# A three-layer kernel on eight cores: another beginning, and six other places at which work is issued

## The reference, cut to what matters

```python
x = L0_attn_hidden_states                     # (4, 4096, 2048) float32
x = x + 0.5 * ffn(layernorm(x))
x = x + attn(layernorm(x))
x = x + 0.5 * ffn(layernorm(x))               # the same weights again

def ffn(x):                                   # D = 2048, K = 8, R = 64
    h = relu(x @ W1 + b1)
    alpha = softmax(h @ W2 + b2)              # 8 weights for each token
    vx = einsum('krd,bsd->bskr', V, x)
    uvx = einsum('kdr,bskr->bskd', U, vx)
    return einsum('bsk,bskd->bsd', alpha, uvx)

def attn(x):                                  # 16 heads of 128
    q, k, v = heads(x @ Wq), heads(x @ Wk), heads(x @ Wv)
    scores = q @ k.T * 128 ** -0.5 + mask     # 0 where |block i - block j| <= 2, blocks of 64; else -1e30
    return merge(softmax(scores) @ v) @ Wo
```

## Time and profile before

| | |
|---|---|
| three runs | 1987.72, 1796.43 and 1979.18 us, median 1979.18 |
| the profiled execution, its own time | 1798.14 us |
| its span (core 0, the slowest) | 1796.6 us |
| spans of the eight cores | 1774.4 to 1796.6 us |
| busy, share of the span | PE 96%, PEld 64%, DVE 44%, ACT 23%, POOL 12% |
| stages on core 0 | first: to 438 us; attention: to 1225; output: to 1449; last: to 1797 |

### The profile page before, as it was taken

One profiled execution on the slowest core, in us unless ns is written; L12 is line 12 of the kernel. 1 busy time (PEld: TensorE's weight loads), 2 busy tenths in 40 slices (PEclk: granted clock), 3 DMA queues, 4 the chain that ended last, 5 costly groups with the idle time before them and its releaser, 6 DMA issues.

```text
span 1796.6 us, 34598 instructions; the slowest of 8 cores (1774.4 to 1796.6 us)
## 1 busy us (share of the span) xinstructions
PE 1726.2 (96%) x12544; PEld 1140.8 (64%) x12544; DVE 786.1 (44%) x1631; ACT 404.8 (23%) x998; POOL 222.4 (12%) x373
## 2 busy tenths in 40 slices
PE   3999899899799999999999999999999999999998
PEld 3876655455577777777777777775444455575555
DVE  5036475344455454545454555545213333153421
ACT  2311311111133333333333333332000011111111
POOL 2001121121111111111111111121000110011000
PEclk9999899999899999999999999999999999999999
DMA  9947877989957574757565556678681553264321
GB/s 210 180 91 229 209 251 176 201 156 182 106 83 103 74 107 76 105 80 94 83 93 94 81 84 81 117 175 254 213 315 49 144 161 127 57 182 129 104 78 55
DMA packets 288583, 242.07 MB, mean 135 GB/s; under 512 B 219808, under 2 KB 260768, under 8 KB 277536
## 3 DMA queue, kind: packets, MB, share of 16 engines
q1 hardware_dynamic: 238096, 121.27, 31.2%
q0 software_dynamic: 44848, 100.19, 29.0%
q10 hardware_dynamic: 5472, 18.40, 3.2%
HBM read 164.74 MB, written 77.07 MB: 135 GB/s over the span
## 4 chain that ended last, share of the span: by engine, by line
PE 85%; DMA 6%; DVE 4%; SPq 2%; issue 1%; ACT 1%; POOL 0%; DVEq 0%; ACTq 0%; POOLq 0%
PE R L745 25%; PE R L390 16%; PE R L735 13%; PE R L1027 12%; PE R L472 4%; PE pX L390 4%; PE R L443 4%; PE R L892 2%; DMA xnTa<-xna 2%; DVE lnb L310 2%; SPq L102 2%; DMA Xa<-x 2%; DMA W1a<-w 2%; PE pX L472 1%; PE pX L852 1%; PE pS L852 1%
## 5 line engine op out<-in xcount | busy, mean ns | idle before, releaser
L735 PE MATMUL R<-wvS,xn2T 128*128 128x256 bf16 x2176 | 253.4, 274 | 6.2 <-ACT Kb L752 6.2
L745 PE MATMUL R<-xn2T,wkS 128*128 128x384 bf16 (+1 forms) x1536 | 251.5, 317 | 0.0
L745 PE MATMUL R<-xn2T,wqS 128*128 128x384 bf16 (+1 forms) x1536 | 239.1, 309 | 0.0
L735 PEld LDWEIGHTS R<-wvS,xn2T 128*128 128x128 bf16 x2176 | 213.2, 98 | 37.5 <-issue 6.5
L390 PE MATMUL R<-xnTa,W1a 128*128 128x256 bf16 (+2 forms) x1632 | 209.1, 288 | 28.5 <-DMA xnTa<-xna 12.6
L1027 PE MATMUL R<-Wo,Ob 128*128 128x512 bf16 x1024 | 222.2, 379 | 0.0
L745 PEld LDWEIGHTS R<-xn2T,wkS 128*128 128x128 bf16 x1536 | 150.1, 98 | 82.1 <-issue 0.6
L745 PEld LDWEIGHTS R<-xn2T,wqS 128*128 128x128 bf16 x1536 | 150.4, 98 | 74.5 <-issue 1.2
L390 PEld LDWEIGHTS R<-xnTa,W1a 128*128 128x128 bf16 x1632 | 142.6, 101 | 77.3 <-issue 34.3
L390 PE MATMUL R<-xnTc,W1c 128*128 128x384 bf16 (+1 forms) x1232 | 185.3, 308 | 0.0
L1027 PEld LDWEIGHTS R<-Wo,Ob 128*128 128x128 bf16 x1024 | 100.1, 98 | 119.6
(11 more groups left out here) (94 smaller groups left out, 1664.1 us busy)
## 6 DMA issues: line engine op xcount, KB each, us to landing
y<-Xc SPq DMA_DIRECT2D x16, 1024.0 KB, 3.9
x1d<-Xa SPq DMA_DIRECT2D x14, 1024.0 KB, 4.3
Xa<-x POOLq DMA_DIRECT2D x10, 1024.0 KB, 10.6
Xc<-x1d POOLq DMA_DIRECT2D x9, 1024.0 KB, 14.9
W1a<-w POOLq DMA_DIRECT2D x16, 512.0 KB, 44.2
w1b<-W1a ACTq DMA_DIRECT2D x16, 512.0 KB, 9.4
wkS<-wk POOLq DMA_DIRECT2D x64, 128.0 KB, 3.6
wqS<-wq POOLq DMA_DIRECT2D x64, 128.0 KB, 4.0
```

Of the source, the lines that this page charges most:

```text
L735: tok = p.mm(lambda e, c=c, o=o: e.matmul(bank[:, 0:256], xn2T[:, o:o + 128], wvS[s][:, c * 256:(c + 1) * 256], start=(c == 0), stop=(c == ...
L745: tok = p.mm(lambda e, c=c: e.matmul(bank[:, 0:w], wS[:, c * 256 + k * 128: c * 256 + (k + 1) * 128], view(xn2T, a * D + c * 128, (D, n), ...
```

## The change

- The beginning. Tile 0 is requested in two halves, and SP requests only tiles 0 and 1. POOL waits for the first half, then requests W1 part 0, W2, tile 2, W1 part 1, tile 3, W1 part 2, tile 4 and the other W1 parts. Tile 0's statistics wait for each half by itself, and its apply and its transpose go by halves (`apply_halves`). All five tiles are normalized first in DVE's list. The pieces of block 0 are written out: each tile is turned in PE's list where it comes, with pieces of one tile for the W1 parts that are there, and pieces of two and three. From e = 5 on the block has two sub-blocks, of three and of two tiles.
- An Exp of one column on ACT is issued at the very beginning.
- Block 1. Tile 0 is normalized a second time during block 0's U matmuls, on ACT (`ln2_act`), and x 7 is requested then. Tile 7 is turned by DMA, not by PE, after item 6 rather than 13. The hooks of block 1 have a new order; tile 10 is normalized on ACT after item 27 and turned after item 29, not during the V matmuls. Four `copy_w1` are issued here.
- Blocks 2 and 3: eight `copy_w1` in block 2 as before, four in block 3, after items 0, 2, 4 and 6, in place of eight.
- The start of attention: one memset of part of `Pn[0]`, ahead of the second normalization of tiles 14 and 15, in place of three whole ones behind it; tile 16's second normalization and transpose one group later, and tile 14's and 15's transposes without it between.
- Loads during attention: in pair 0 the next pair's slab parts come in groups 2 to 5, six in each, rather than in groups 1 to 5; no `cast_wo` in pair 0, six in each of pairs 1 to 6 (before five in each of 0 to 6).
- The last stage's groups 1 and 2 change places.

```diff
-BLOCKS = [[(0, 1), (1, 2), (3, 2)], [(5, 2), (7, 1)], [(8, 3)], [(11, 3)], [(14, 3)]]
+BLOCKS = [[(0, 3), (3, 2)], [(5, 2), (7, 1)], [(8, 3)], [(11, 3)], [(14, 3)]]
...
+    p.op("scalar", lambda e: e.activation(warm[:, :], mhalf[:, :], AF.Exp), cst["mhalf"])
...
-                    st[:, j * 6:j * 6 + 6], x[:, j * 512:(j + 1) * 512]), token, *free)
+                    st[:, j * 6:j * 6 + 6], x[:, j * 512:(j + 1) * 512]),
+                    token[j // 2] if isinstance(token, list) else token, *free)
...
+        def apply_halves(self, x, st_tok):
+            st, stok = st_tok
+            b, free = self.xn.take()
+            toks = [p.op("vector", lambda e, o=o: e.tensor_scalar(
+                b[:, o:o + 1024], x[:, o:o + 1024], st[:, 24:25], st[:, 26:27],
+                ALU.subtract, ALU.mult), stok, *free) for o in (0, 1024)]
+            ln_sets.give(st, toks[1])
+            return b, toks
...
-                    8, [tok])
+                    8, [tok[half] if isinstance(tok, list) else tok])
...
-    for t in range(5):
-        load_x(t, "sync")
+    x0_tok = [p.dma("sync", S(f"dxa{h}_x0"), xa(0)[:, h * 1024:(h + 1) * 1024],
+                    rows(dx, 0)[:, h * 1024:(h + 1) * 1024]) for h in range(2)]
+    load_x(1, "sync")
     W1atok = []
+    p.wait("gpsimd", x0_tok[0])
     for e in range(16):
         W1atok.append(p.dma("gpsimd", S(f"w1a{e}"), W1a[e][:, :], rows(dw1, e)))
         if e == 0:
             cst["w2p"] = p.dma("gpsimd", S("c_w2p"), W2b[:, :], dw2[:, :])
+        if e < 3:
+            load_x(e + 2, "gpsimd")
...
-        if t < 5 or t == 7:
+        if t < 5:
             xnT_tok[t] = norm.turn(*norm_b[t], xnTa, place[t], free)
...
+    def ln2_act(t, new):
+        st = norm.shift(*norm.stats(xa(t), x_add[t], minus=True))
+        ln2_b[t] = b, tok = norm.apply_act(xa(t), st)
+        x_free[t % 7] = (tok, x1_tok[t])
+        load_x(new, "gpsimd")
...
-    for t in range(3):
+    st0 = norm.stats(xa(0), x0_tok)
+    norm_b[0] = norm.apply_halves(xa(0), st0)
+    for t in range(1, 5):
         ln1(t)
         flush_ln()
-    ln1_turn(0)
-    ln1(3)
-    flush_ln()
-    items = [(0, 0), (0, 1), (0, 2)]
-    items += [(1, e) for e in range(3)] + [(s, e) for e in (3, 4) for s in (0, 1)]
-    items += [(2, e) for e in range(5)]
-    items += [(s, e) for e in range(5, 16) for s in range(3)]
-    hooks = at_hooks([(1, call(ln1_turn, 1)), (1, call(ln1, 4)), (1, flush_ln), (2, call(ln1_turn, 2)),
-                      (7, call(ln1_turn, 3)), (9, call(ln1_turn, 4)),
-                      (36, call(ln1, 5)), (39, call(ln1, 6)), (41, flush_ln)])
-    run_items(0, items, hooks)
-    vu_a(0, at_hooks([(("v", 1), call(ln1_turn, 5)), (("v", 2), call(ln1_turn, 6))]))
+    items = [(0,), (0, 1, 0), (1,), (1, 1, 0), (0, 2, 1), (2,), (2, 1, 0), (2, 1, 1), (0, 3, 2),
+             (3,), (0, 3, 3), (3, 1, 0), (3, 1, 1), (3, 1, 2), (4,), (0, 3, 4),
+             (4, 1, 0), (4, 1, 1), (4, 1, 2), (3, 2, 3), (3, 2, 4)]
+    items += [(t, n, e) for e in range(5, 16) for t, n in ((0, 3), (3, 2))]
+    late = {len(items) - 8: call(ln1, 5), len(items) - 4: call(ln1, 6), len(items) - 2: flush_ln}
+    for i, item in enumerate(items):
+        if len(item) == 1:
+            ln1_turn(item[0])
+        else:
+            t, n, e = item
+            first.w1(0, t, n, place[t], e, [xnT_tok[q] for q in range(t, t + n)])
+        if i in late:
+            late[i]()
+    vu_a(0, at_hooks([(("v", 1), call(ln1_turn, 5)), (("v", 2), call(ln1_turn, 6)),
+                      (("u", 0), lambda: ln2_act(0, 7))]))
...
-    for t in range(3):
-        ln2_load(t, 7 + t)
-    flush_ln()
+    ln1_half(7)
+    ln2_load(1, 8)
+    ln2_load(2, 9)
...
-        (4, call(ln2_store, 0)), (7, call(ln2_store, 1)), (9, call(ln2_store, 2)),
-        (9, call(ln1_half, 7)), (10, call(ln2_load, 3, 10)), (10, flush_ln),
-        (11, call(ln1_act, 7)), (11, call(ln1_half, 8)), (13, call(ln1_turn, 7)),
-        (13, call(ln2_load, 4, 11)), (13, flush_ln), (17, call(ln1_act, 8)),
-        (18, call(ln2_store, 3)), (20, call(ln1_turn, 8)), (22, call(ln1_half, 9)),
-        (23, call(ln2_store, 4)), (26, call(ln1_act, 9)), (27, call(ln1_half, 10)),
-        (29, call(ln1_turn, 9)), (31, call(ln1_act, 10))]
-        + [(3 + 4 * i - i // 7, call(copy_vu, i)) for i in range(8)])
+        (1, call(ln2_store, 0)), (2, call(ln2_load, 3, 10)), (3, call(ln2_load, 4, 11)), (3, flush_ln),
+        (4, call(ln1_half, 8)), (5, call(ln1_act, 7)), (6, call(ln1_turn, 7)),
+        (7, call(ln2_store, 1)), (9, call(ln2_store, 2)), (9, call(ln1_half, 9)),
+        (11, call(ln2_store, 3)), (13, call(ln2_store, 4)), (15, call(ln1_half, 10)),
+        (18, call(ln1_act, 8)), (20, call(ln1_turn, 8)), (22, call(ln1_act, 9)),
+        (24, call(ln1_turn, 9)), (27, call(ln1_act, 10)), (29, call(ln1_turn, 10))]
+        + [(3 + 4 * i - i // 7, call(copy_vu, i)) for i in range(8)]
+        + [(5 + 8 * i, call(copy_w1, i)) for i in range(4)])
     run_items(1, items, hooks)
-    vu_a(1, at_hooks([(("v", 1), call(ln1_turn, 10))]))
+    vu_a(1, {})
...
-        if blk in (2, 3):
-            pairs += [(2 * i + 1, call(copy_w1, 8 * (blk - 2) + i)) for i in range(8)]
+        if blk == 2:
+            pairs += [(2 * i + 1, call(copy_w1, 4 + i)) for i in range(8)]
+        if blk == 3:
+            pairs += [(2 * i, call(copy_w1, 12 + i)) for i in range(4)]
...
     p.stage("attention")
-    ln2(14)
-    ln2(15)
-    flush_ln()
...
-    for b in range(3):
-        p.op("vector", lambda e, b=b: e.memset(Pn[b][:, :], 0.0))
+    p.op("vector", lambda e: e.memset(view(Pn[0], 0, (384, 2), (1, 128)), 0.0))
+    ln2(14)
+    ln2(15)
+    flush_ln()
...
-                if pr < PAIRS - 1 and g > 0 and n % 2 == 0:
-                    for q in range(2 if n == 0 else 1):
-                        if parts_due:
-                            load_slab(*parts_due.popleft(), proj_done[(pr, g)])
-                if pr < PAIRS - 1 and g == 0 and n < 5 and wo_casts:
+                if pr == 0 and g > 1:
+                    due = int(n < 6)
+                else:
+                    due = 0 if pr in (0, PAIRS - 1) or g == 0 or n % 2 else 2 if n == 0 else 1
+                for q in range(due):
+                    if parts_due:
+                        load_slab(*parts_due.popleft(), proj_done[(pr, g)])
+                if 0 < pr < PAIRS - 1 and g == 0 and n < 6 and wo_casts:
                     cast_wo(*wo_casts.popleft(), proj_done[(pr, g)])
...
-                if pr == 0 and g == 0:
-                    if n == 3:
+                if (pr, g) == (0, 0) and n in (3, 5):
+                    turn_xn2({3: 14, 5: 15}[n], last_v)
+                if (pr, g) == (0, 1) and n in (2, 5):
+                    if n == 2:
                         ln2(16)
                         flush_ln()
-                        turn_xn2(14, last_v)
-                    if n == 5:
-                        turn_xn2(15, last_v)
-                    if n == 6:
+                    else:
                         turn_xn2(16, last_v)
...
-    ORDER = [3, 4, 5, 0, 2, 1]
+    ORDER = [3, 4, 5, 0, 1, 2]
```

More of the change, by code:

```diff
@@ L257, in build_nc @@
     mhalf = tiny("mhalf", 1, F32)
+    warm = tiny("warm", 1, F32)
     lgb = tiny("lgb", 40, F32)
```

## The result

The changed kernel takes 1780.61 us (median of 4 runs, 1778.68 to 1782.2; the profiled one 1780.48). Its ratio to the kernel before is 0.9913, 95% interval 0.9893 to 0.9932: 0.9% faster, where I forecast 2.0%.

A forecast was written before the change was run, and what follows sets the result against it. The prediction took the kernel as TensorE-bound (PE busy 96%), with only PE's waits and low-clock work to win. Terms of 7 + 4 + 5 + 8.5 + 10.5 + 2.8 = 37.8 us gave 1760.3 on core 0; forecast 1762, eight-in-ten range 1750 to 1781.

The forecast's parts named there:

- B: Block 1: an earlier second normalization and tile 7 turned by DMA gain 4 us (bounds -3 to 9.7).
- What bounds it: Whole kernel: PE is busy 96% of the span; a reordering can win only its waits and low-clock work.
- The step from the sum to the time: Whole kernel: core 0's 37.8 us gain gives 1760.3; cores draw together, one keeps a transfer wait, so 1762 us.
- Core 3's check: Cross-check on core 3, whose transfer waits are small: the terms leave 1755.4 us of span, 1756.9 as a time.
- C: End of block 1: tile 10 turned at item 29 instead of in the V phase gains 5 us (0 to 6.3).
- A: Beginning, up to block 0's V phase: first transpose later, W1 waits gone, V phase at 108; gain 7 us.
- E: Start of attention: K copy and probabilities' transpose waits go; gain 10.5 us (4 to 16).
- rival 1: Waits move to transfers, tiles 10 and 16 still late: 1773 us, or 1778 with less gained at attention's start; chance 0.20.
- D: Block 3: four W1 copies taken out of its end remove a transpose wait; gain 8.5 us (2 to 10.2).
- F: Last groups: the last group gets three tiles, hiding its first transpose; gain 2.8 us (0 to 3).
- Rivals 3 and 4: Everything overlaps, about 1748 us, chance 0.06; or PE stays at 1.2 GHz through the beginning, 1822 us, chance 0.04.
- Rival 2: Beginning gives nothing because of POOL's 22 issues or a low clock: 1769 us, 1780 with part of rival 1; chance 0.10.

The follow-up runs named there:

- 3: Changed kernel with the powers of tiles 0 and 1 among POOL's requests instead of behind all 22; ratio to before 0.9886, median 1774.39 us.
- Experiment 4: Changed kernel with the z transpose issued ahead of the U group whose x1 store it stood behind; ratio to before 0.9928, median 1777.95 us.
- Experiment 5: Changed kernel with tiles 8, 9 and 10 normalized by DVE at items 8, 10 and 16 of block 1, not by ACT; one comparable time, 1772.96 us.
- 6: Changed kernel with the sixteen W1 copies back in blocks 2 and 3, eight each, none in block 1; ratio to before 0.99, median 1780.57 us.
- kernel 8: Changed kernel with the edits of 3, Experiment 4, Experiment 5 and 7 together; two times, 1769.5 and 1774.64 us, no interval.
- 10: kernel 8 with six of eight V and U copies moved from block 1 into block 0's V phase; ratio to before 0.9809, median 1761.36 us.
- 9: Changed kernel with six of eight V and U copies moved from block 1 into block 0's V phase; ratio to before 0.9919, median 1779.61 us.
- 2: Kernel before with the changed kernel's beginning alone; ratio to before 0.9972, median 1788.15 us.
- 7: Changed kernel with tile 16's statistics one item later in the first head pair; ratio to before 0.9882, median 1777.02 us.
- 12: 10 with four V copies issued ahead of the softmax, two U copies at the last V and first U group; ratio to before 0.9842, median 1766.74 us.

## Why the prediction failed, step by step

The time lies on the side "within 2%", to which I gave 0.59, and 0.4 us inside the upper edge of the range (1781), which is luck: the working has a price for neither of the two errors that brought it there. The forecast of 1762 was 18.6 us too low. Of that 7.0 is the sum (37.8 forecast on core 0, 30.8 gained; B alone is 7.1 short), and 13.0 that core 0 (1765.8) is not the last core (1778.8), less the 2 us that I had added for it.

**What bounds it** held: PE is still at 97%, and nearly all that changed is its waits and its slow pieces. **The step from the sum to the time** failed. I took the gain of core 0, the slowest before, and corrected by 2 us for "the cores draw together". Core 0 was slowest before since it had long waits of each kind that the change removes (9.5, 8.8, 7.0); core 2, which sets the time after, had no probabilities' wait to lose (805.6 before, 805.7 after in that stretch). Core 3's check summed to 1755.4; it measured 1773.7: of these 18.3 us, B and C, taken as a gain of 4, were a loss of 9.5 (151.5 to 161.0 from V to V), A gave 4.9 for 7, E was a loss of 1.1 for 2.5, and block 3, taken at nothing, a loss of 1.3.

**A**: 7 forecast, 7.6 on core 0, 4.2 on the mean. The later first transpose was right in kind: "18.3" is 13.5 behind the half's landing, measured 14.0. The landing itself was taken too early (4.8; 6.6 on the mean), so the transpose came at 20.6 on the mean. That POOL's issues are on the path is shown by 3: 7.9 us.

**B is the term that failed**: +4 forecast, -3.1 measured on core 0 and -5.1 on the mean. Its gross gain, 8.4 (9.7 if ACT never blocks), was nearly right: with the new waits taken away (8) the block takes 78.1 to 79.1 on four cores, some 8 less than before. Two prices were wrong.
- "So nothing; uncovered they would cost 3.7": tile 0's added statistics on DVE. They were uncovered, and the wait is 3.9 on the mean. I had looked for cover at PE (the filler piece and the banks), but the damage runs through SP's order: the z transpose comes behind the x1 store and behind x 7's request. Experiment 4 removes the wait for 4.9 with the statistics still in their place.
- "PE stands about 2.5 us at item 20. Tiles 9 and 10 cost some 1 each": tile 8's came nearly as worked out (2.15 to 2.17 on every core). Tiles 9 and 10 were 3.7 together on the mean (2.1 to 5.9), where DVE's row shows x 9 landing late, and each stop brings slow pieces, which I had not counted. Experiment 5 removes all three for 8.8 in block 1, of which 2.9 comes back in block 2. My own bound ("-3 if each waits 4 us") was too narrow, because it held no z wait at all.

**C**: 5 forecast, 3.4 on core 0, -1.6 on the mean. What I had wrong is the wait's cause. I looked at how long one transpose takes (12 to 20 us against 10 us of V phase), and tile 10's took 8.2 on core 2; but it was issued 9.3 us after its tile was ready, behind the issues of tile 8's and 9's. Copies have a part in it: with four fewer in block 1 (6) the wait goes from 4.4 to 2.2, and with six fewer on kernel 8 from 7.8 to 0.8 (10), while the same six taken from the changed kernel (9) leave it at 4.4. Why they matter in one order and not in the other stays open. So rival 1 (0.20, 1773 to 1778) happened in part: in C, and larger in B than its 2, but D did not shrink to 3 and no wait for tile 16's transpose came. Its argument against, "copies only left block 3", overlooked that they had gone to block 1, as I had written myself in B.

**D**: 8.5 forecast, 10.3 on core 0, 6.6 on the mean; the wait is gone on all cores. 6 ties about 2 us of it to the copies: with them put back the stretch grew by 2.1 of the 6.6 that it had lost. Another 3.4 is the difference between before's profiled execution (70.1) and 2 (66.7), in which D's places are those of before; whether the new beginning or chance between executions gave it, no run shows.

**E**: 10.5 forecast with 11.1 worked out, for a core that had the probabilities' wait of 7.0. Cores 0, 4 and 5 had it and gained 8.8, 15.0 and 11.6. The other five had 805.3 to 805.6 and have 803.7 to 807.1: no gain, or 1.7 at most. The step that failed was to take core 0's wait for every core's. On four of these five (2, 3, 6 and 7) there is a second reason: between 500 us and 950 us PE now waits 1 to 4 times for a probabilities' transpose or for DVE, 1.9 to 3.7 us a core in all, and not once on any core before. "The Wo casts have 36 places for 32 in pairs 1 to 6: nothing" and the slab parts' new places stand in that stretch; no run tests whether they are the cause. The Qb wait, forecast at 3.5, is 3.80 on all cores; and one item's shift (7) would have saved 6.2.

**F**: 2.8 forecast, 3.4 on core 0 and 3.9 on the mean. **Rivals 3 and 4** did not occur: the waits did not all go, and PE was out of the low clock by 48 us. **Rival 2** did in part: POOL's issues do stand in front of the first power (7.9 us by 3), and yet the beginning gave 4.2 on the mean. That "together with a part of rival 1, 1780" is the measured time is chance, since it counts A as nothing.

## What to carry to other kernels

When statistics or a normalization are moved between other work on an engine, follow each store that waits for what is behind them, and then what stands behind that store in its own queue: the price was paid in another queue (3.9 us a core), where PE's own cover did not help. Where the transfer engines are busy all the time in one stretch, copies moved into it from a stretch with a wait move the wait too (6); look for a stretch with an empty share instead (0.05 to 0.21 at 100 to 110 us in kernels 8, 9 and 10). The copies issued there (12) left a z wait of 0.8, where 10 had 4.2, though the time was no better. And sum on the core that will be last after the change, not on the one that is last before.

## What the runs showed of the hardware that I had not expected

- Halving the first tile brought its first half in only 0.7 to 2.3 us sooner than the whole tile on the same core before (7.90 against 8.81 on core 2, 6.52 against 7.84 on core 0), and on five cores the second half landed at 10.0 to 10.4, later than the whole tile had.
- The last z transpose of block 0 took 4.4 to 5.0 us to landing on the eight cores before, and 8.4 to 10.6 after, where 1 MB had been requested 1.4 us ahead from another engine's queue. The Trainium skill (DMA: Bandwidth & Descriptors, "Issuing engines are not separate DMA queues") says that transfers of all issuing engines run on the same 16 engines and interleave; the pair of numbers agrees.
- The issue of one DMA transpose of a whole tile held SP for 11 to 19 us where the transfer share was near 1 or above (tiles 8 and 9 on core 2 after, tile 8 in 5 and 8), tile 10's behind them for 6.1, against 2.1 to 3.4 us for tile 7's, issued at 160 to 166 us in the changed kernel; whatever stands behind it is as late. The share alone doesn't set it: at 217.64, at a share of 1.09, three z transposes of a quarter of the size held SP for 3.87 together.
- Between the cores of one execution of the same program tile 7's transpose took 6.0 to 26.6 us to land in 10 and 9.7 to 35.3 in 12. The time is that of the slowest core, which is why a mean gain of 25 us over the changed kernel (10: 1747.3 against 1772.0) came out as 21.
